# A token tower with top-4 expert layers on one core: routing pieces moved between the slots of the first expert phase, second-layer matrices loaded later

## The reference

```
h = h + attention(layernorm(h))
x = layernorm(h)                                    # 2368 x 192
logits_f, logits_r = (x @ W + b) @ normalised_emb.T # 128 experts each
w_f, w_r = softmax, top 4 kept, renormalised
mid = sum over the 4 chosen n of  w_f[n] * (x   @ f_know[n])   # 192 -> 128
out = sum over the 4 chosen n of  w_r[n] * (mid @ r_know[n])   # 128 -> 192
return h + out
```

## Time and profile before

| | |
|---|---|
| median of 3 runs | 823.0 us (820.96 to 825.43) |
| profiled execution | 822.98 us, span 821.3 us |
| mean granted TensorE clock | 0.856 of 2.4 GHz |
| busy, share of the span | PE 75%, DVE 46%, ACT 44%, POOL 49% |
| DMA | 147.13 MB, mean 179 GB/s |

### The profile page before, as it was taken

One profiled execution on the slowest core, in us unless ns is written; L12 is line 12 of the kernel. 1 busy time (PEld: TensorE's weight loads), 2 busy tenths in 40 slices (PEclk: granted clock), 3 DMA queues, 4 the chain that ended last, 5 costly groups with the idle time before them and its releaser, 6 DMA issues.

```text
span 821.3 us, 14397 instructions
## 1 busy us (share of the span) xinstructions
PE 615.0 (75%) x4572; PEld 517.9 (63%) x4572; DVE 378.1 (46%) x1337; ACT 359.1 (44%) x760; POOL 400.6 (49%) x397
## 2 busy tenths in 40 slices
PE   6798998989998874575999999988199804998000
PEld 5586876868787653343999889877187603676000
DVE  2846678879597999966930011110011110231132
ACT  4337285574757362234344434433047502576000
POOL 2433260523423056620773067774477773771674
PEclk9789999999998997655999999989599956999555
DMA  5253729476440675891577567799989724897432
GB/s 137 58 194 121 257 76 356 133 281 233 147 199 21 119 162 129 220 219 30 168 219 184 134 183 200 208 316 342 259 224 255 201 65 109 243 269 199 129 96 69
DMA packets 139574, 147.13 MB, mean 179 GB/s; under 512 B 12025, under 2 KB 123042, under 8 KB 139490
## 3 DMA queue, kind: packets, MB, share of 16 engines
q1 hardware_dynamic: 126114, 118.63, 50.2%
q0 software_dynamic: 13376, 27.41, 11.5%
HBM read 73.50 MB, written 72.50 MB: 178 GB/s over the span
## 4 chain that ended last, share of the span: by engine, by line
PE 41%; DVE 20%; POOL 11%; issue 11%; ACT 8%; DMA 6%; SPq 2%; POOLq 0%; DVEq 0%; ACTq 0%
PE bank L1231 19%; POOL gat L772 7%; PE bank L921 5%; PE bank L1219 5%; ACT qk_pad L1337 4%; POOL mid_dram L780 4%; DVE pick L2004 3%; PE bank L968 3%; DMA gat<-wide_dram,slots 2%; DMA wide_dram<-os_pair 2%; PE bank L1240 2%; DVE smax L1778 2%; PE bank L906 1%; DVE probs L1781 1%; PE bank L985 1%
## 5 line engine op out<-in xcount | busy, mean ns | idle before, releaser
L1231 PE MATMUL bank<-matrices,xsT 96*64 (+1 forms) x1632 | 224.6, 295 | 0.0
L1231 PEld LDWEIGHTS bank<-matrices,xsT 96*64 96x64 f32 (+1 forms) x1632 | 192.8, 139 | 23.1 <-issue 5.7
L772 POOL DMA_INDIRECT gat<-wide_dram,slots x152 | 145.9, 960 | 124.4 <-SPq L606 77.0
L757 POOL DMA_INDIRECT wide_dram<-x2b,slots x76 | 75.0, 987 | 84.0 <-issue 42.6
L2052 DVE TENSOR_SCALAR acc<-gat,wts 128x128 f32<-128x128 f32 x19 | 6.1, 319 | 231.7 <-DMA gat<-wide_dram,slots 231.7
L714 POOL TENSOR_TENSOR qk_sum<-qk_pad 64x888 f32<-64x888 f32 x16 | 26.8, 1676 | 155.5 <-ACT qk_pad L1337 139.0
L1548 ACT ACTIVATE os_pair<-bank 64x384 f32<-64x384 f32 x136 | 58.5, 478 | 72.3 <-DMA wide_dram<-os_pair 36.9
L780 POOL DMA_INDIRECT mid_dram<-comb,slots x76 | 74.0, 974 | 27.8 <-issue 21.6
L1561 ACT ACTIVATE xsT<-bank 96x512 f32<-96x512 f32 (+1 forms) x136 | 59.6, 487 | 58.2 <-PE bank L1219 56.8
L1542 ACT ACTIVATE os_pair<-bank 64x512 f32<-64x512 f32 x68 | 40.3, 592 | 85.3 <-PE bank L1231 79.1
L921 PE MATMUL bank<-tok_wT,pixT 128*128 128x192 f32 x384 | 70.6, 345 | 1.3 <-ACT pixT L1314 1.3
(11 more groups left out here) (196 smaller groups left out, 914.9 us busy)
## 6 DMA issues: line engine op xcount, KB each, us to landing
wide_dram<-zeros SPq DMA_DIRECT2D x6, 3328.0 KB, 14.0
mid_dram<-zeros SPq DMA_DIRECT2D x8, 1664.0 KB, 17.7
xs<-wide_dram SPq DMA_DIRECT2D x68, 192.0 KB, 3.1
wide_dram<-os_pair SPq DMA_DIRECT2D x68, 192.0 KB, 3.7
matrices<-in_L_ffn_f_know SPq DMA_DIRECT2D x8, 1536.0 KB, 15.2
matrices<-in_L_ffn_r_know SPq DMA_DIRECT2D x8, 1536.0 KB, 12.2
wide_dram<-os_pair SPq DMA_DIRECT2D x68, 128.0 KB, 2.8
xs<-mid_dram SPq DMA_DIRECT2D x68, 128.0 KB, 4.0
```

Of the source, the lines that this page charges most:

```text
L757: pool.indirect_dma_start(wide_dram[b], bass.IndirectOffsetOnAxis(ap=slots[:, t, e:e + 1], axis=0), x2b[:, t - BATCHES[b][0], :], None)\
L772: pool.indirect_dma_start(gat[i][:, e, :], None, wide_dram[b], bass.IndirectOffsetOnAxis(ap=slots[:, t, k:k + 1], axis=0))\
L1231: last = pe.matmul(out_bank[0:W, n * width:(n + 1) * width], xsT[r][0:kp, c:c + W], matrices[0:kp, bass.ds(starts[(r * SB + k) * 2 + half] ...
```

## The change

- TensorE and ScalarE run only pieces 0 to 2 ahead of phase 0. Pieces 3 to 10 run inside phase 0, one behind each of the first eight slots (behind `products(s, r)` on TensorE, behind `results(s, r)` on ScalarE).
- The warm-up products ahead of phases 0 and 1 are gone (WARM 24, 20 become 0, 0).
- The first layer's last chunk is issued behind phase 0's first four row loads instead of ahead of them.
- No second-layer chunk is loaded inside phase 1: all 8 are issued behind it, the first ahead of `expert_end(1)`, and TensorE waits for all of them behind phase 2's warm-up. The three VectorE instructions that found the half point go, and phase 1's loop on SP is written out like that of the other phases.

```diff
-WARM = (24, 20, 24, 16)
+WARM = (0, 0, 24, 16)
-ROUTED = 11
+PIECES, ROUTED = 11, 3
-FREED = EXPERTS // 2
-EARLY = FREED * 256 // (CHUNK * D)
...
@@ sync
-            load_f(range(6, EXPERTS // CHUNK))
+            load_f(range(6, 7))
...
-                if ph == 1:
-                    half = sp.value_load(half_used[0:1, 0:1], min_val=2, max_val=STEPS)
-                    with sp.Fori(2, STEPS) as s, sp.If(s < half):
-                        next_rows(s)
-                    for n in range(EARLY):
-                        with sp.If(half + n < used):
-                            s = half + n
-                            s.max_val = STEPS - 1
-                            next_rows(s)
-                        if n == 0:
-                            sp.wait_ge(y_filled[ph], half * RING)
-                        load_r(n, r_early)
...
-                else:
-                    each_step(sp, used, 2, next_rows)
+                each_step(sp, used, 2, next_rows)
...
             for r in range(RING):
                 load_rows(0, 0, r)
+            load_f(range(7, 8))
             expert_rows(0, rows_of_second)
             expert_end(0)
...
             expert_rows(1, None)
-            load_r(EARLY, r_late[0])
+            load_r(0)
             expert_end(1)
-            for n in range(1, EXPERTS // CHUNK - EARLY):
-                load_r(EARLY + n, r_late[n])
+            for n in range(1, EXPERTS // CHUNK):
+                load_r(n)
@@ tensor
                 for n in range(WARM[ph]):
                     pe.matmul(bank[0][:, 0:ROWS], ident[:], ones[:], start=True, stop=True)
                 if ph == 2:
-                    pe.wait_ge(r_late[-1], 16)
+                    pe.wait_ge(r_loaded, 16 * (EXPERTS // CHUNK))
...
                         for r in (2 * q, 2 * q + 1):
                             products(s, r, starts)
+                            k = ROUTED + s * RING + r
+                            if ph == 0 and k < PIECES:
+                                piece(k)
...
-                if ph == 2:
-                    pe.wait_ge(r_early, 16 * EARLY)
-                    for landed in r_late[:-1]:
-                        pe.wait_ge(landed, 16)
@@ vector, plan part 3
-                    if b == 1:
-                        link(dve.tensor_scalar(half_has[:], ...
-                        link(dve.tensor_reduce(half_f[:], ...
-                        link(dve.tensor_scalar(half_used[:], ...
```

More of the change, by code:

```diff
@@ L152, in tower @@
         steps_f = sb("steps_f", [1, 2])
-        half_has = sb("half_has", [1, STEPS])
-        half_f = sb("half_f", [1, 1])
-        half_used = sb("half_used", [1, 1], I32)
         steps_used = sb("steps_used", [1, 2, 2], I32)
@@ L364, in tower @@
         end_copied = sem("end_copied")
-        r_early = sem("r_early")
-        r_late = [sem(f"r_late{n}") for n in range(EXPERTS // CHUNK - EARLY)]
+        r_loaded = sem("r_loaded")
         xs_loaded = [[sem(f"xs_loaded{p}_{r}") for r in range(RING)] for p in range(4)]
@@ L531, in load_rows, with load_r @@
                   .then_inc(xs_loaded[ph][r], 16)
-            def load_r(n, landed):
+            def load_r(n):
                 dst = matrices[:, n * CHUNK * D:(n + 1) * CHUNK * D].rearrange("p (n k) -> p n k", k=D)
-                sp.dma_start(dst, r_view[:, n * CHUNK:(n + 1) * CHUNK, :]).then_inc(landed, 16)
+                sp.dma_start(dst, r_view[:, n * CHUNK:(n + 1) * CHUNK, :]).then_inc(r_loaded, 16)
             def expert_rows(ph, ahead):
@@ L1167, in end_logits, with piece @@
                 return pe.matmul(bank[7][:, c:c + 256], x2T[t % 3][0:DH, 1, :], r_mat[0:DH, 1, :], start=False, stop=True)
-            def ahead(k):
+            def piece(k):
                 if k == 0:
@@ L1201, in _ @@
             for k in range(ROUTED):
-                ahead(k)
+                piece(k)
             def experts(ph):
```

## The result

| | before | after |
|---|---|---|
| median of the runs, us | 823.7 (820.96 to 825.43, 4 runs) | 798.8 (794.91 to 803.26, 4 runs) |
| ratio, 95% interval | | 0.970 [0.964, 0.976] |
| profiled execution, us | 822.98 | 803.26 |
| its span, us | 821.3 | 801.5 |

802 had been forecast; it is 798.8. A second set of runs on one chip gave 800.42 against 824.45, ratio 0.972 [0.968, 0.976]. All runs of this document are in the chip's faster state but two of e3_warm_back's six (810.16 and 811.53 us), which its ratio leaves out.

The account below looks back on a forecast made before the run. POOL's chain was taken to decide, b=1's start setting phase 3 (TensorE largest part, 41%). Starting b=1 at 560, not 581.01, takes 21 us off the 821.3 span: 800.3, plus 1.7 around it, 802.0 us; range 796 to 810, 8-in-10 range 794 to 815.

Parts of the forecast that it names:

- Phase 0's start: TensorE's first transposes of phase 0 at 369.6 in place of 395.6, after 2.34 us of register loads.
- The pieces: Pieces 3 to 10 inside phase 0 cost TensorE 6 us, plus 1 us of stall (0 to 4).
- The clock: Without warm-up, phase 0's first matrices run at 1.2 GHz until the clock is granted: 3 us lost.
- Rival B: The clock stays at 1.2 GHz through phase 0's interleaved slots: 823 us, nothing gained; chance 0.08.
- Piece 10, scatter, hand-over: Piece 10 ends at 399.8, b=1's scatter at 455.4; after a 12.2 us hand-over POOL starts b=0 at 467.6.
- Rival A: With piece 10 4 us earlier, the scatter is done before SP asks, no late hand-over: 793 us; chance 0.10.
- Phase 1: TensorE starts 12 us earlier and saves 9 us without early loads: phase 1 ends at 553.6 instead of 574.6.
- b=1 on POOL: POOL begins b=1 at 560 in place of 581.01; its 103.8 us stay unchanged.
- The late load: Eight chunks behind phase 1 take 52 us, loaded at 610; phase 2 ends at 667, its cover used up but holding.
- Behind POOL's b=1: SP goes on at 665.2 in place of 686.19, 21 us earlier, and releases phase 3's rows.

Follow-up runs that it names:

- e3_warm_back: The changed kernel with the warm-ups of phases 0 and 1 put back (24 and 20): 803.17 us, ratio 0.972.
- c0_after: The changed kernel itself with no edit, timed for reference on the second set's chip: 800.42 us, ratio 0.972.
- e4: The changed kernel with SP's last stores of a phase ahead of the wait for the next phase's rows: 792.42 us, ratio 0.962.
- e7: The changed kernel with SP's last stores, the wait for them and POOL's release ahead of the wait for the next rows: 789.28 us, ratio 0.958.
- e1: The kernel before with only the second-layer loads moved, all eight chunks behind phase 1: 811.2 us, ratio 0.984.
- e2: The kernel before with only the pieces, their warm-ups and the last feature chunk changed, early loads kept: 812.38 us, ratio 0.987.
- e6: The changed kernel with four late chunks loaded a second time and phase 2 waiting for all twelve: 821.46 us, ratio 0.996.
- e8: e7 with phase 3's warm-up ahead of TensorE's wait for the combined rows: 791.16 us, ratio 0.961.
- e9: The changed kernel with all 11 routing pieces ahead of phase 0 again: 1027.01 us, ratio 0.976, in the set where the kernel before took 1051.44.

## Why the prediction was right, step by step

The profile after is set against the steps less 2.4 us, by which its attention part took longer (the marks). The mechanism held: POOL's chain decides, the hand-over behind the scatter is what comes late next, and the late load stays just covered. The sizes on the path were off by 1 to 3 us each, in both directions, so that the sum comes this near is in part luck; the load's landing was off by 9.5 us, which its cover hid.

- *Phase 0's start.* Forecast 369.6, came at 369.62 − 2.4 = 367.2. The 2.34 us of idle that I had put down to register loads did not follow: there is no gap ahead of the first transposes, nor in the other profiles of this order. 2.4 us better.
- *The pieces.* From the first transposes to piece 10's end 29.2 us (398.83 − 369.62), of which 20.1 are phase 0's own (the terms of my 20.2 add up to that): 9.1 for pieces and stalls, where I had 7. The pieces' own products take 6.0, as I had said; it is the stall that I had too small, 3.1 in place of 1. Visible parts of it are 1.49 us for ScalarE and 1.23 for rows (the slowest of the rows loaded there took 10.5 us to land, near the 12.2 that I gave as worst for them).
- *The clock.* The 3 us for a cold start were not paid in this profile: 0.54 in 366:370 means 1.00 for its last 0.3 us only, so the clock rose as phase 0's first transposes began (369.62), ahead of its first product (373.28), and the warm-ups of e3 brought it no sooner. Rival B did not happen in any profile. But the grant could still be lost: in c0_after the clock fell back behind an idle of 1.54 us for rows (0.50 in 376:378) and was 1.00 again from 379, which cost some 1.7 us (1.95 for eight transposes and 2.75 for sixteen products, 1.04 and 1.96 at full clock). By the Trainium skill, "TensorE: Matmul & The Clock Gate", section "Part 4: PE-mode transpose", these transposes should have held the grant back. The traces do not bear this out: it came with the first of them here, and 1.4 us into them in c0_after (from 363.93; 0.84 in 364:368, 1.00 in 366:368). The test is a weak one, since piece 2's products stand just ahead.
- *Piece 10, scatter, hand-over.* 396.4 (399.8), scatter from 401.3 to 451.9 (404.8 to 455.4), POOL's b=0 at 465.2 (467.6): 3.5 us better into the hand-over, which took 13.3 us in place of 12.2. That SP's wait for the scatter would be late next, at the price shown at phase 2's end, was the least obvious step, and e4 and e7 confirm it by taking it away. Rival A did not happen, and its condition was far too mild: 3.4 us of the 4 that it asks for came, yet the gap is the full one. SP had issued its last store of the loop at 440.64 and then stood 13.0 us for the scatter (next issue at 456.70); by my estimate the whole gain of A needs the scatter some 9 us earlier (467.66 less 454.61, phase 0's end, and 4.3).
- *Phase 1.* Rows for its start and for step 1 at 457.9 and 470.3 (461, 471), no other wait for rows inside; its end 549.2 (553.6). e1 and e2 show both terms: no loads beside it, and an earlier start.
- *b=1 on POOL.* 557.8 (560), with no gap; POOL itself and not phase 1 set it (92.6 us for b=0, forecast 91). Its own 103.5 us did not stretch beside the load, with the DMA engines at 1.09 in 575:600 (103.8 before).
- *The late load.* 12.6 MB in 49.8 us (553.13 to 602.89), 253 GB/s against the assumed 242; loaded at 600.5 (610), phase 2 over at 659.6 (667). The late load's cover is small as said: TensorE idle 4.83 us before phase 3, and of e6's 27.6 us of delay 19.5 are paid.
- *Behind POOL's b=1.* SP on at 663.8 (665.2). Its hand-over took 13.8 us in place of 12.2, which gives 1.6 of the gain back.

Sum by the mark: 22.2 us where I had 21. The median of the runs fell by 24.9 (24.0 in the second set), 2 to 3 us more than the profiled executions show by the mark. I did not find where; single profiles of a kernel lie up to 5 us from its median.

## What to carry to other kernels

Work on latency (small matmuls that answer to another engine) belongs between dense products on TensorE, not ahead of them: 18.0 us at half clock at the front became 9 us at full clock among the slots. That is what this case shows; how much of it the order gives, and how much the warm-ups' going, was not separated. Before moving work down, follow what its last result releases and which in-order queue waits for that: here SP's stores of a finished phase stood behind a wait for the scatter, and putting them first gave 8 us more by the medians and 11 by the mark, the larger part at a hand-over that the kernel before had too. A transfer put into a hole is free only as long as its landing stays ahead of the engine that now ends the hole; measure that cover by making it longer.

## What was not expected of the hardware

- The clock. In the kernel before it stayed at 0.50 through piece 2 and the pieces behind it, with TensorE busy 7.78 of 7.80 us (364:371.8) and then 7.73 of 14 (371:385). In the eight profiles with pieces 0 to 2 alone at the front (after, c0, e2, e3, e4, e6, e7, e8) it rose 3.2 to 5.1 us behind the mark, with phase 0's first transposes or warm-ups behind piece 2 in place of pieces. In e1, where the pieces stand in front again, 24 warm-ups from 383.83 took 8.18 us; the clock was 0.61 over 383:391 and 1.00 from 389.5. Why dense routing products brought no grant is open.
- Ahead of phase 0 TensorE stood 2.34 us in the kernel before, with nothing that it waited for the earlier trace rows, and not at all in the changed kernel. I take this for register loads that a full queue hides; no run shows it.
- POOL's indirect DMAs kept their pace of 1.27 us each while the DMA engines stood at 1.09 of their time and moved 339 GB/s.
- The same kernel took 823 and 1051 us in different sets. In the second TensorE was idle for 126 us in e9 with nothing that it waited for, often 1 to 3 us ahead of single products, and 54.3 us for ScalarE's copies of the transposes (5.7 in the changed kernel), while a product's duration hardly changed (313 ns in place of 296). The mean granted clock was 0.76 to 0.78 there, in the kernel before as well, and 0.84 to 0.87 in the other sets. Where that comes from is open.
